# Experts of a hybrid network on one core: turning of the gates, second biases and their addition one half later, store one half later

## The chip, the cores and the metric

The kernel runs on one core of a Trainium2 chip. The metric is the device time in microseconds (us). Engines: PE (TensorE, matmuls and transposes; its weight loads are shown as PEld), DVE (VectorE), ACT (ScalarE), POOL (GpSimd) and SP (SyncE, which here only issues DMAs). Each engine works through a queue of its own in program order, and they wait for each other through semaphores.

## The reference

Eight pictures of 128 channels by 32 x 32 points pass through three layers. The first is an attention over the 1024 points of a picture, the second a state-space layer (a scan over the points), the third a mixture of eight experts. The change lies wholly in the third. Of the reference this is what matters (`t` holds the 1024 tokens of each picture, 128 values each):

```python
t = t + _L1_ffn_ref(_ln_t(t), router_w, w1, b1, w2, b2)

def _moe(tokens, router_w, w1, b1, w2, b2):
    logits = tokens @ router_w.T
    probs = softmax(logits)
    rw, re = top_k(probs, 2)
    rw = rw / maximum(rw.sum(-1), 1e-12)
    combine = zeros((N, 8)).at[arange(N)[:, None], re].set(rw)
    out = tokens
    for e in range(8):
        h = gelu(tokens @ w1[e] + b1[e])
        y = h @ w2[e] + b2[e]
        out = out + combine[:, e:e + 1] * y
    return out
```

All eight experts are computed for every token, in the reference and in the kernel. The second biases enter as `combine @ b2`.

## The kernel before

The three layers run one after the other over the eight pictures; the experts fill the last quarter of the program, from about 746 us. For each picture `b` the work of the experts is cut into 16 halves: half `n` is expert `n // 2` on tokens `512 * (n % 2)` and following. A half goes through these steps:

- PE, `expert` (lines 778 to 780): first product, three matmuls of 512 columns (high and low parts), into bank 4 or 5. It is issued two halves ahead.
- ACT, `gelu` (line 1378): the activation, into `hid[n % 2]`.
- PE, `second` (line 1028): second product, four matmuls, into bank 3, 6 or 7 in turn (half 15 uses bank 6, as half 13 does). It waits until `gelu` of that half is done and until DVE has added the half that used the bank before.
- DVE, `experts` (line 1970): four instructions add the gated product to `acc`. Each half added raises `e_added`.

So PE alternates: `second(n)`, `expert(n + 2)`, `second(n + 1)`, `expert(n + 3)`, and so on; `expert` of the last two positions belongs to the next picture. Below, 0', 1', ... are halves of the picture that follows in time.

Between the halves stands the preparation of the next picture, `b + 1`. In order: DVE takes the statistics of its tokens (after half 0), POOL makes the factors of the norm out of them (`norm`, lines 604 to 608), ACT normalizes (`token_norm`, line 1359, after half 5), PE turns the tokens (line 1040, after half 5), ACT and DVE split them into high and low parts (lines 1366 and 1896), PE computes the logits (after half 7), DVE finds the two largest and the gates (lines 1902 to 1938, after halves 7, 8, 10 and 11; the last writes `comb_s` and raises `e_gates_ready`). Then come the steps that the change moves:

- PE, `turn_weights` (line 1059): transposes the gates into bank 2. It waits for `e_gates_ready`.
- DVE, `turned` (line 1944): copies them to `comb_t` and raises `e_gates_copied`.
- PE, `second_biases` (line 1067): four matmuls of 512 columns, the gates times the second biases, into banks 0 and 1 (`lo_banks`). It waits for `e_gates_copied`.
- DVE, `biases` (line 1953): adds them to the next picture's `acc`.

The output of the picture before is turned by PE (`turn_out`, line 1077, after half 1; it waits for all 16 halves of that picture) into the same two banks, and ACT copies it to `o_ch` (`store`, line 1385), from where SP stores it to memory.

The order of every engine is written out by hand. Which step stands after which half is set by the comparisons `if n == ...` in the `experts` function of PE and ACT, and by the tuple of slots in that of DVE, which names the half after which each of the eight parts of `scores` runs: statistics, low, largest, places, softmax, weights, turned, biases. For the first picture these parts run inside the scan, by other lists, which stay as they are; so `experts` issues the turning seven times, for pictures 1 to 7.

Of the kernel before, what the change touches and what calls it, by code (L numbers as in the profile page):

```python
# [16 lines left out]
def hybrid_kernel(nc, x, x_tok, wqk, bqk, wv, bv_rows, wo2, bo, ident, fold, group_mean,  # L17
# [37 lines left out]
    with ExitStack() as ctx:  # L55
# [582 lines left out]
        def _(pe):  # L638
# [368 lines left out]
            def expert(b, u, n):  # L1007

                e, h = n // 2, n % 2
                if n >= 2 or not isinstance(b, int) or b > 0:  # L1010
                    pe.wait_ge(e_hidden_ready, 2 * NE * b + n - 1)
                pe.wait_ge(e_low_ready, b + 1)
                r = slice(h * BANK, (h + 1) * BANK)
                split(ps[:, 4 + n % 2, :], (w1_h[:, e, :], w1_l[:, e, :]),
                      (uh[u][:, r], ul[u][:, r])).then_inc(e_hidden_product, 1)

            def second(b, n, first):

                e, h = n // 2, n % 2
                pe.wait_ge(e_hidden_ready, 2 * NE * b + n + 1)  # L1020

                before = 3 if n < 2 * NE - 1 else 2
                if n >= 3:
                    pe.wait_ge(e_added, 2 * NE * b + n - before + 1)
                elif not first:
                    pe.wait_ge(e_added, 2 * NE * b - (3, 0, 1)[n])
                for t in range(4):
                    last = nc.tensor.matmul(ps[:, Y_BANKS[n], t * P:(t + 1) * P], hid[n % 2][:, t * P:(t + 1) * P],  # L1028
                                            w2_f[:, e, :], start=True, stop=True)
                last.then_inc(e_second_product, 1)  # L1030

            def turn_tokens(b):

                pe.wait_ge(e_normed, b + 1)
                if not isinstance(b, int) or b > 1:
                    pe.wait_ge(e_out_ready, b - 1)
                elif b == 1:
                    pe.wait_ge(e_bias_added, 1)
                for t in range(NT):
                    last = nc.tensor.transpose(cols(lo_banks, t, P), un[:, t, :], id_f[:])  # L1040
                last.then_inc(e_turned, 1)

            def logits(b, u):

                pe.wait_ge(e_low_ready, b + 1)
                if not isinstance(b, int) or b > 0:
                    pe.wait_ge(e_gates_copied, b)
                for t in range(NT):
                    r = slice(t * P, (t + 1) * P)
                    o = ps[:, 2, 2 * t * NE:2 * (t + 1) * NE]  # L1050
                    nc.tensor.matmul(o, uh[u][:, r], rw_s[:].rearrange("p k e -> p (k e)"), start=True, stop=False)
                    last = nc.tensor.matmul(o, ul[u][:, r], rw_s[:].rearrange("p k e -> p (k e)"), start=False, stop=True)
                last.then_inc(e_logits, 1)

            def turn_weights(b, u):

                pe.wait_ge(e_gates_ready, b + 1)
                pe.sem_inc(wait_carrier, 1)
                nc.tensor.transpose(ps[:, 2, P:2 * P], comb_s[u][:].rearrange("p k t e -> p (k t e)"),
                                    id_f[:]).then_inc(e_gates_turned, 1)  # L1060

            def second_biases(b):

                pe.wait_ge(e_gates_copied, b + 1)
                for h in range(2):
                    for part in range(2):
                        last = nc.tensor.matmul(lo_banks[:, h, :], comb_t[:], b2_s[:, part, h * BANK:(h + 1) * BANK],
                                                start=(part == 0), stop=(part == 1))
                last.then_inc(e_bias_product, 1)

            def turn_out(b, u):

                pe.wait_ge(e_added, 2 * NE * b + 2 * NE)
                if not isinstance(b, int) or b < B - 1:
                    pe.wait_ge(e_bias_added, b + 2)
                for t in range(NT):
                    done = nc.tensor.transpose(cols(lo_banks, t, P), acc[u][:, t, :], id_f[:])
                done.then_inc(e_sum_turned, 1)

            def experts(b, u, first, last):  # L1080
                for n in range(2 * NE):
                    second(b, n, first)
                    if n + 2 < 2 * NE:
                        expert(b, u, n + 2)
                    elif not last:
                        expert(b + 1, 1 - u, n + 2 - 2 * NE)
                    if n == 1 and not first:
                        turn_out(b - 1, 1 - u)
                    if not last:
                        if n == 5:  # L1090
                            turn_tokens(b + 1)
                        if n == 7:
                            logits(b + 1, 1 - u)
                        if n == 12:
                            turn_weights(b + 1, 1 - u)
                        if n == 13:
                            second_biases(b + 1)

            pe.wait_ge(attn_weights_loaded, 16 * 9)
# [49 lines left out]
        def _(act):  # L1149
# [202 lines left out]
            def token_norm(b):  # L1352

                act.wait_ge(e_shift_ready, 2 * b + 2)
                if not isinstance(b, int) or b > 0:
                    act.wait_ge(e_sum_started, b)
                    act.wait_ge(e_turned, b)
                for t in range(NT):
                    last = nc.scalar.activation(un[:, t, :], X[:, b, t * P:(t + 1) * P], ACT.Identity,  # L1359
                                                bias=enb[:, t:t + 1], scale=ers[:, t:t + 1])  # L1360
                last.then_inc(e_normed, 1)

            def token_high(b, u):

                act.wait_ge(e_turned, b + 1)
                nc.scalar.activation(two(uh[u][:]), lo_banks, ACT.Copy).then_inc(e_high_ready, 1)
# [6 lines left out]
            def gelu(b, n):  # L1373

                act.wait_ge(e_hidden_product, 2 * NE * b + n + 1)
                if n >= 2 or not isinstance(b, int) or b > 0:
                    act.wait_ge(e_second_product, 2 * NE * b + n - 1)
                nc.scalar.activation(hid[n % 2][:], ps[:, 4 + n % 2, :], ACT.Gelu,  # L1378
                                     bias=b1_f[:, n // 2:n // 2 + 1]).then_inc(e_hidden_ready, 1)

            def store(b, u):

                act.wait_ge(e_sum_turned, b + 1)
                act.wait_ge(out_free, b + 1)
                nc.scalar.activation(two(o_ch[u][:]), lo_banks, ACT.Copy).then_inc(e_out_ready, 1)

            def experts(b, u, first, last):
                for n in range(2, 2 * NE):
                    gelu(b, n)
                    if n == 3 and not first:  # L1390
                        store(b - 1, 1 - u)
                    if not last:
                        if n == 5:
                            token_norm(b + 1)
                        if n == 7:
                            token_high(b + 1, 1 - u)
                        if n == 9:
                            gate_exponentials(b + 1)
                if not last:
                    gelu(b + 1, 0)  # L1400
                    gelu(b + 1, 1)
# [40 lines left out]
        def _(dve):  # L1442
# [513 lines left out]

            def experts(b, u, first, last):

                parts = dict(zip((0, 5, 7, 8, 10, 11, 12, 13), scores(b + 1, 1 - u))) if not last else {}
                dve.wait_ge(e_bias_added, b + 1)  # L1960
                dve.wait_ge(e_gates_ready, b + 1)
                for k in range(2 * NE):
                    e, h = k // 2, k % 2
                    dve.wait_ge(e_second_product, 2 * NE * b + k + 1)
                    if k >= 2:
                        dve.wait_ge(e_added, 2 * NE * b + k - 1)
                    bank = (3, 6, 7)[k % 3] if k < 2 * NE - 1 else 6
                    for t in range(4):
                        tt = 4 * h + t
                        done = nc.vector.scalar_tensor_tensor(acc[u][:, tt, :], ps[:, bank, t * P:(t + 1) * P],  # L1970
                                                              comb[u][:, tt, e:e + 1], acc[u][:, tt, :],
                                                              ALU.mult, ALU.add)
                    done.then_inc(e_added, 1)
                    if k in parts:
                        parts[k]()
# [119 lines left out]
```

## Time and profile before

| | |
|---|---|
| median of 3 runs | 1012.92 us |
| lowest, highest | 1011.82, 1015.36 us |
| profiled execution, span | 1012.5 us |
| PE busy | 879.7 us, 87% |
| DVE busy | 740.6 us, 73% |
| ACT busy | 522.8 us, 52% |
| POOL busy | 250.1 us, 25% |
| mean granted TensorE clock | 0.938 |

The span runs from the first to the last instruction of one profiled execution; the profile states no other time of that execution than this span. A row of a timeline gives the start, the length, the engine and line, what is written and what is read, and in brackets how long the engine had been idle and who released it. Lengths of matmuls that follow each other overlap, so the distance from start to start tells how long one holds the engine. Shares of busy time are averages over the whole program; here only the stretch of the experts matters.

### The profile page before, as it was taken

What the parts mean: (1) busy time and instruction counts of PE and PEld (TensorE: products, weight loads), DVE (VectorE), ACT (ScalarE), POOL (GpSimd) and SP (SyncE); (2) the same over time, 40 slices, a digit from 0 to 9 for tenths busy, and PEclk for the clock granted to TensorE, in tenths of its full rate; (3) what the DMA queues carried; (4) which work ended last, traced back from release to release, by engine and by line L of the source; (5) the groups of instructions that cost most, each with busy time, mean ns of one, the idle gap of its engine ahead of it and who ended that gap; (6) DMA issues with size and microseconds to landing.
All of it is one profiled execution on the core that took longest, in us unless ns stands there. A gap on an engine that the chain in (4) does not pass through costs nothing.

```text
span 1012.5 us, 19616 instructions
## 1 busy us (share of the span) xinstructions
PE 879.7 (87%) x7534; PEld 686.5 (68%) x7534; DVE 740.6 (73%) x1959; ACT 522.8 (52%) x796; POOL 250.1 (25%) x250
## 2 busy tenths in 40 slices
PE   3788999999988797979787979798779899989997
PEld 2556565656575675867566767676568788878887
DVE  2867677767766768696859595856968877878785
ACT  1525445544577465646464646453334665456543
POOL 0035111011100534343325252527520111011100
PEclk9879999999999697989799989899999999999999
DMA  5531000000003030302030303031000000000000
GB/s 146 177 134 22 11 11 21 22 11 12 21 1 67 7 73 5 70 20 54 10 64 2 73 2 73 2 73 64 2 1 1 22 22 22 1 22 22 22 3 40
DMA packets 30892, 36.13 MB, mean 36 GB/s; under 512 B 4560, under 2 KB 24912, under 8 KB 30800
## 3 DMA queue, kind: packets, MB, share of 16 engines
q1 hardware_dynamic: 29648, 30.68, 12.4%
q10 hardware_dynamic: 1152, 4.19, 1.1%
q8 instruction: 61, 1.00, 0.4%
q14 instruction: 31, 0.25, 0.1%
HBM read 21.50 MB, written 4.98 MB: 26 GB/s over the span
## 4 chain that ended last, share of the span: by engine, by line
PE 60%; DVE 25%; ACT 6%; issue 5%; POOL 2%; SPq 0%; DMA 0%; DVEq 0%; ACTq 0%; POOLq 0%
PE ps L1028 7%; PE ps L699 6%; DVE cacc L1693 4%; PE ps L950 4%; PE ps L686 4%; PE ps L778 3%; DVE acc L1970 3%; PE ps L780 3%; PE ps L779 3%; PE ps L653 3%; PE ps L941 2%; PE ps L658 2%; ACT un L1359 2%; PE ps L934 2%; PE ps L675 2%
## 5 line engine op out<-in xcount | busy, mean ns | idle before, releaser
L1970 DVE SCALAR_TENSOR_TENSOR acc<-ps,comb,acc 128x128 f32<-128x128 f32 x512 | 141.2, 344 | 22.2 <-PE ps L1028 21.7
L1028 PEld LDWEIGHTS ps<-w_f,hid 128*128 128x128 f32 x1024 | 131.2, 191 | 16.2 <-ACT hid L1378 8.0
L1378 ACT ACTIVATE hid<-ps,b_f 128x512 f32<-128x512 f32 x128 | 86.1, 685 | 107.5 <-PE ps L780 107.4
L1028 PE MATMUL ps<-w_f,hid 128*128 128x128 f32 x1024 | 136.8, 276 | 4.6 <-ACT hid L1378 4.6
L569 POOL TENSOR_TENSOR srs<-sve,neg_half 128x1 f32<-128x1 f32 x64 | 50.8, 794 | 217.3 <-DVE gram L1802 217.3
L1550 DVE TENSOR_REDUCE nmax<-ps 128x1 f32<-128x1024 f32 x64 | 78.1, 1221 | 30.7 <-PE ps L658 30.4
L1693 DVE SCALAR_TENSOR_TENSOR cacc<-ps,cw,cacc 128x1023 f32<-128x1023 f32 (+5 forms) x72 | 91.8, 1275 | 10.4 <-ACT cacc L1250 9.6
L1319 ACT ACTIVATE dcy<-ps 128x1024 f32<-128x1024 f32 x64 | 65.0, 1016 | 59.0 <-PE ps L901 58.9
L1166 ACT ACTIVATE probs<-ps,nmax 128x1024 f32<-128x1024 f32 x64 | 71.2, 1113 | 38.7 <-DVE nmax L1550 35.8
L1785 DVE SCALAR_TENSOR_TENSOR dcy<-dcy,g_sb 128x1024 f32<-128x1024 f32 x64 | 86.1, 1346 | 0.1
L686 PEld LDWEIGHTS ps<-id_f,probs 128*128 128x128 f32 x512 | 59.9, 144 | 33.1 <-issue 23.5
L1172 ACT ACTIVATE pt<-ps 128x512 f32<-128x512 f32 x64 | 38.1, 595 | 77.4 <-PE ps L686 76.9
L686 PE MATMUL ps<-id_f,probs 128*128 128x128 f32 x512 | 69.8, 280 | 8.8 <-ACT pt L1172 6.7
L950 PE MATMUL ps<-y_w 128*128 128x256 f32 x256 | 74.4, 417 | 3.3 <-DVE X L1812 2.8
L1845 DVE TENSOR_TENSOR y_w<-ps,zs 128x256 f32<-128x256 f32 x64 | 27.0, 422 | 64.4 <-PE ps L941 46.8
L517 POOL TENSOR_TENSOR rs<-bve,neg_half 128x16 f32<-128x16 f32 x8 | 23.2, 2901 | 166.0 <-DVE bve L1598 166.0
L1555 DVE COPY pt<-ps 128x512 f32<-128x512 f32 x64 | 43.9, 686 | 27.7 <-PE ps L686 27.4
L699 PE MATMUL ps<-pt,v_f 128*64 128x512 f32 x256 | 64.1, 615 | 0.0
L950 PEld LDWEIGHTS ps<-y_w 128*128 128x128 f32 x256 | 51.7, 208 | 15.7 <-issue 2.9
L778 PE MATMUL ps<-uh,w_h 128*128 128x512 f32 x128 | 61.1, 477 | 0.0
L653 PE MATMUL ps<-k_a,q_a 128*128 128x512 f32 x128 | 48.5, 462 | 6.1 <-ACT probs L1166 4.4
L1250 ACT ACTIVATE cacc<-ps,cb,cw 128x1024 f32<-128x1024 f32 x24 | 28.9, 1204 | 48.0 <-PE ps L780 47.9
(212 smaller groups left out, 1905.0 us busy)
## 6 DMA issues: line engine op xcount, KB each, us to landing
c_dec<-exp_dram SPq DMA_DIRECT2D x32, 256.0 KB, 5.2
xc<-in_x SPq DMA_DIRECT2D x8, 512.0 KB, 3.6
q_b<-q_a SPq DMA_DIRECT2D x16, 256.0 KB, 2.8
X<-in_x_tok ACTq DMA_DIRECT2D x8, 512.0 KB, 5.5
c_rep<-cacc SPq DMA_DIRECT2D x32, 128.0 KB, 3.1
out<-o_ch SPq DMA_DIRECT2D x8, 512.0 KB, 2.6
w_f<-in_w SPq DMA_DIRECT2D x2, 512.0 KB, 4.2
cst_f<-in_sel_rows SPq DMA_DIRECT2D x1, 512.0 KB, 4.5
```

Source lines behind the costliest of these rows:

```text
L653: nc.tensor.matmul(S[j % 2][:, h, :], q_a[u][:, j * P:(j + 1) * P], k_a[u][:, h * BANK:(h + 1) * BANK], start=True, stop=False)
L686: last = nc.tensor.transpose(T[:, h, k * P:(k + 1) * P], probs[:, j % 2, (4 * h + k) * P:(4 * h + k + 1) * P], id_f[:])
L699: last = nc.tensor.matmul(O[e * DV:(e + 1) * DV, h, :], v_f[u][:, k, :], pt[:, k, h * BANK:(h + 1) * BANK], start=(quarter == 0), stop=(qu ...
L778: nc.tensor.matmul(o, lhs[0], rhs[0], start=True, stop=False)
L950: last = nc.tensor.matmul(ps[:, 6 + n % 2, DI:BANK].rearrange("p (k t) -> p k t", k=2), y_w[:, g, k, :], y_w[:, g, k:5:4 - k, :], start=(g ...
L1028: last = nc.tensor.matmul(ps[:, Y_BANKS[n], t * P:(t + 1) * P], hid[n % 2][:, t * P:(t + 1) * P], w2_f[:, e, :], start=True, stop=True)
L1166: nc.scalar.activation(probs[:, j % 2, :].rearrange("p (a n) -> p a n", a=2), S[j % 2], ACT.Exp, bias=nmax[:, j:j + 1], accum_out=rsum[u][ ...
L1378: nc.scalar.activation(hid[n % 2][:], ps[:, 4 + n % 2, :], ACT.Gelu, bias=b1_f[:, n // 2:n // 2 + 1]).then_inc(e_hidden_ready, 1)
L1550: nc.vector.tensor_reduce(nmax[:, j:j + 1], S[j % 2], AX_XY, ALU.max, negate=True).then_inc(max_ready, 1)
L1693: ins = nc.vector.scalar_tensor_tensor(cacc[b % 3][0:rows, g, k:N], banks[:, 0:N - k], cw[0:rows, g, DCONV - 1 - k:DCONV - k], cacc[b % 3] ...
L1785: nc.vector.scalar_tensor_tensor(mix[n % 3][:], dcy[n % 3][:], 1.0, g_sb[u][:, c:c + 1, :].to_broadcast([P, NH, P]), ALU.min, ALU.mult).th ...
L1970: done = nc.vector.scalar_tensor_tensor(acc[u][:, tt, :], ps[:, bank, t * P:(t + 1) * P], comb[u][:, tt, e:e + 1], acc[u][:, tt, :], ALU.m ...
```

## The change

Four numbers change. In the experts of every picture, PE turns the next picture's gates after half 13 where it did so after half 12, and computes the second biases after half 14 where it did so after half 13. DVE adds these biases after half 14 where it did so after half 13; its copy of the turned gates stays after half 12. ACT stores the output of the picture before after half 4 where it did so after half 3.

```diff
@@ PE, experts
                         if n == 7:
                             logits(b + 1, 1 - u)
-                        if n == 12:
+                        if n == 13:
                             turn_weights(b + 1, 1 - u)
-                        if n == 13:
+                        if n == 14:
                             second_biases(b + 1)
@@ ACT, experts
                     gelu(b, n)
-                    if n == 3 and not first:
+                    if n == 4 and not first:
                         store(b - 1, 1 - u)
@@ DVE, experts
-                parts = dict(zip((0, 5, 7, 8, 10, 11, 12, 13), scores(b + 1, 1 - u))) if not last else {}
+                parts = dict(zip((0, 5, 7, 8, 10, 11, 12, 14), scores(b + 1, 1 - u))) if not last else {}
```

On PE, around the turning of the gates (line 1059) in the first picture's experts; `hid` and `w_f` are the operands of a second product, `uh`, `ul`, `w_h`, `w_l` those of a first product:

```order
 L780 MATMUL ps<-uh,w_l 128x512
+L1028 MATMUL ps<-w_f,hid 128x128 x4
+L778 MATMUL ps<-uh,w_h 128x512
+L779 MATMUL ps<-ul,w_h 128x512
+L780 MATMUL ps<-uh,w_l 128x512
 L1059 MATMUL ps<-id_f,comb_s 128x128
 L1028 MATMUL ps<-w_f,hid 128x128 x4
```

A second product and a first product (half 13, and half 15 ahead) now stand in front of the turning. The same pair leaves the place behind the biases; farther on, before the output of the picture before is turned (line 1077):

```order
 L779 MATMUL ps<-ul,w_h 128x512
 L780 MATMUL ps<-uh,w_l 128x512
-L1028 MATMUL ps<-w_f,hid 128x128 x4
-L778 MATMUL ps<-uh,w_h 128x512
-L779 MATMUL ps<-ul,w_h 128x512
-L780 MATMUL ps<-uh,w_l 128x512
 L1077 MATMUL ps<-id_f,acc 128x128 x8
 L1028 MATMUL ps<-w_f,hid 128x128 x4
```

The turning, the pair behind it and the four matmuls of the biases keep their order among themselves; they have moved back by one pair as a block.

On DVE, from the sum of half 12 to the statistics of the picture after; line 1944 copies the turned gates and line 1953 adds the biases:

```order
 L1970 SCALAR_TENSOR_TENSOR acc<-ps,comb,acc 128x128 x4
 L1944 CAST comb_t<-ps 128x128
-L1970 SCALAR_TENSOR_TENSOR acc<-ps,comb,acc 128x128 x4
+L1970 SCALAR_TENSOR_TENSOR acc<-ps,comb,acc 128x128 x8
 L1953 TENSOR_TENSOR acc<-ps,acc 128x1024
-L1970 SCALAR_TENSOR_TENSOR acc<-ps,comb,acc 128x128 x12
+L1970 SCALAR_TENSOR_TENSOR acc<-ps,comb,acc 128x128 x8
 L1886 BN_STATS est<-X 128x6 x8
```

The addition of the biases has moved from between the sums of halves 13 and 14 to between those of 14 and 15. The copy has not moved.

On ACT, from the exponentials of the gates (`tex`) to the token norm (`un`), before:

```order
L1371 ACTIVATE tex<-tsh 128x64
L1378 ACT_TABLE_LOAD
L1378 ACTIVATE hid<-ps,b_f 128x512 x10
L1385 ACTIVATE o_ch<-ps 128x1024
L1378 ACTIVATE hid<-ps,b_f 128x512 x2
L1359 ACTIVATE un<-X,enb,ers 128x128 x8
L1378 ACTIVATE hid<-ps,b_f 128x512 x2
```

and now:

```order
L1371 ACTIVATE tex<-tsh 128x64
L1378 ACT_TABLE_LOAD
L1378 ACTIVATE hid<-ps,b_f 128x512 x11
L1385 ACTIVATE o_ch<-ps 128x1024
L1378 ACTIVATE hid<-ps,b_f 128x512
L1359 ACTIVATE un<-X,enb,ers 128x128 x8
L1378 ACTIVATE hid<-ps,b_f 128x512 x2
```

The copy to `o_ch` now stands between the activations of halves 4 and 5, of which the latter is the last ahead of the token norm.

## Rows read from the trace of the kernel before

**Rows 1.** The page, part 1: busy time and share of each engine.
```profile
PE 879.7 (87%) x7534; PEld 686.5 (68%) x7534; DVE 740.6 (73%) x1959; ACT 522.8 (52%) x796; POOL 250.1 (25%) x250
```

**Rows 2.** Busy time by engine in one picture's stretch, granted clock, DMA share, GB/s.
```profile
841.00:874.50 33.50, 30.79 (x213) 27.45 (x213) 27.40 (x128) 18.61 (x29) 4.41 (x4) 1.00 0.04 17
```

**Rows 3.** Waits from 775 to 978 us: total, times, longest.
```profile
PE ps L1059 <- DVE comb_s L1938: 9.1, 6, 1.5
PE ps L1040 <- ACT un L1359: 4.0, 6, 0.7
```

**Rows 4.** Idle time before line 1059, from 774 to 975 us: total, times.
```profile
  DVE comb_s L1938: 10.7, 7
```

**Rows 5.** Timeline of PE around a turning: start, length, operation, [idle before, releaser].
```profile
872.77 0.40 PE L780 MATMUL ps<-uh,w_l 128*128 128x512 f32 x1
874.69 0.30 PE L1059 MATMUL ps<-id_f,comb_s 128*128 128x128 f32 x1 [1.52 <-DVE comb_s L1938]
874.84 1.13 PE L1028 MATMUL ps<-w_f,hid 128*128 128x128 f32 x8
875.73 0.48 PE L778 MATMUL ps<-uh,w_h 128*128 128x512 f32 x1
876.27 0.39 PE L780 MATMUL ps<-uh,w_l 128*128 128x512 f32 x1
876.50 1.08 PE L1067 MATMUL ps<-b_s,comb_t 128*128 128x512 f32 x4
877.43 1.05 PE L1028 MATMUL ps<-w_f,hid 128*128 128x128 f32 x8
879.02 1.05 PE L1028 MATMUL ps<-w_f,hid 128*128 128x128 f32 x8
```

**Rows 6.** Timeline of DVE, the same stretch and the start of the next picture.
```profile
874.32 0.22 DVE L1938 TENSOR_TENSOR comb_s<-comb,comb_h 128x64 f32<-128x64 f32 x1
874.46 1.12 DVE L1970 SCALAR_TENSOR_TENSOR acc<-ps,comb,acc 128x128 f32<-128x128 f32 x4
875.50 0.28 DVE L1944 CAST comb_t<-ps 128x128 fp32r<-128x128 f32 x1
876.01 1.13 DVE L1970 SCALAR_TENSOR_TENSOR acc<-ps,comb,acc 128x128 f32<-128x128 f32 x4 [0.23 <-PE ps L1028]
877.69 1.23 DVE L1953 TENSOR_TENSOR acc<-ps,acc 128x1024 f32<-128x1024 f32 x1 [0.56 <-PE ps L1067]
878.84 1.12 DVE L1970 SCALAR_TENSOR_TENSOR acc<-ps,comb,acc 128x128 f32<-128x128 f32 x4
880.11 1.13 DVE L1970 SCALAR_TENSOR_TENSOR acc<-ps,comb,acc 128x128 f32<-128x128 f32 x4 [0.16 <-PE ps L1028]
881.79 1.12 DVE L1970 SCALAR_TENSOR_TENSOR acc<-ps,comb,acc 128x128 f32<-128x128 f32 x4 [0.56 <-PE ps L1028]
...
885.37 3.19 DVE L1970 SCALAR_TENSOR_TENSOR acc<-ps,comb,acc 128x128 f32<-128x128 f32 x12
```

**Rows 7.** Timeline of ACT: four halves' activations, the store, the token norm.
```profile
871.61 0.69 ACT L1378 ACTIVATE hid<-ps,b_f 128x512 f32<-128x512 f32 x1 [0.91 <-PE ps L780]
...
884.85 1.02 ACT L1385 ACTIVATE o_ch<-ps 128x1024 f32<-128x1024 f32 x1 [0.18 <-PE ps L1077]
886.43 0.69 ACT L1378 ACTIVATE hid<-ps,b_f 128x512 f32<-128x512 f32 x1 [0.56 <-PE ps L780]
888.02 0.69 ACT L1378 ACTIVATE hid<-ps,b_f 128x512 f32<-128x512 f32 x1 [0.90 <-PE ps L780]
888.60 3.18 ACT L1359 ACTIVATE un<-X,enb,ers 128x128 f32<-128x128 f32 x8
```

**Rows 8.** Timeline of ACT in the scan: two 128x1024 activations in a row.
```profile
719.42 1.02 ACT L1366 ACTIVATE uh<-ps 128x1024 fp32r<-128x1024 f32 x1 [0.34 <-PE ps L1040]
720.34 1.02 ACT L1319 ACTIVATE dcy<-ps 128x1024 f32<-128x1024 f32 x1
```

**Rows 9.** Timeline of POOL: the last step of the token norm's factors.
```profile
887.54 0.20 POOL L608 TENSOR_TENSOR enb<-enb,neg_one 128x8 f32<-128x8 f32 x1
```


## The prediction

> **What bounds the kernel now.** I began with the page's busy times: PE is the busiest engine over the program [rows 1], but that is an average over three layers, and the change lies in the last. So I cut the experts into one stretch per picture with the view by windows. In such a stretch (841.0 to 874.5 us) PE is busy 30.8 us, DVE 27.4, ACT 18.6, and TensorE is granted its full clock, 1.00 (2.4 GHz) [rows 2]. PE therefore sets the pace, and what a change is worth is read from PE's idle time. The view of waits names that: per picture PE waits 1.5 us for the gates at line 1059 and 0.7 us for the normalized tokens at line 1040 [rows 3]. The first is the one that the change touches. It occurs in all seven pictures of the experts, 10.7 us of shown idle time together [rows 4].
>
> The timeline shows why. The last matmul of the pair ahead of the turning starts at 872.77 [rows 5]. One such matmul holds PE for 876.50 - 876.27 = 0.23 us [rows 5], so PE is free at 873.00. The turning needs `comb_s`, which DVE begins to write for the last time at 874.32 and has ready at 874.54 [rows 6]. The turning starts at 874.69. So PE stands still for 1.69 us in front of it (the row shows 1.52, since it counts from the modelled end of the last matmul). Behind the turning in PE's queue stands half 13, which needs nothing of the gates.
>
> **PE: the turning one pair later.** What half 13 needs is there before 873.00. Its activation starts at 871.61 [rows 7] and takes 0.69, so it ends at 872.30. Its bank was last read by the sum of half 10, which DVE has done before it works on the gates. The half's weights and inputs are long loaded. So at 873.00 PE now starts the pair (second product 13, first product 15). A pair not held up takes 879.02 - 877.43 = 1.59 us [rows 5]. It ends at 874.59. The turning is still let go by the gates at 874.69, since nothing in front of them on DVE moves. PE idles 0.10 us where it idled 1.69. The turning holds PE for 0.15 us (874.84 - 874.69), as before.
>
> From 874.84 on the kernel before runs pair (13, 15), the biases, pair (14, 0'), pair (15, 1'), pair (0', 2'). The changed kernel runs pair (14, 0'), the biases, pair (15, 1'), pair (0', 2'). The durations: the pair behind the turning 876.50 - 874.84 = 1.66, the biases 877.43 - 876.50 = 0.93 [rows 5]. So half 15 starts at 877.43, half 0' at 879.02 and half 1' at 880.61. Before, half 0' started one pair after half 15, that is 879.02 + 1.59 = 880.61. The gain is one pair, 1.59 us for each picture, if no other wait appears. Seven pictures give 11.1 us.
>
> **What is late next: DVE.** This is where the gain could be lost, because the pairs now come sooner than DVE's sums were paced before. I follow DVE's queue. The sum of half 12 starts at 874.46, the copy of the turned gates at 875.50 [rows 6], so one sum of four instructions holds DVE for 1.04 us. The turning ends at 874.69 + 0.30, ahead of 875.50: the copy does not wait, though PE issues the turning after half 13 now and DVE's copy stays ahead of half 13. The copy takes 0.28. Then:
> - sum 13: at 875.78, without the 0.23 us wait that the row has [rows 6], since its product was made before the turning. It ends its hold at 876.82.
> - sum 14: its product is ready 876.01 - 874.84 = 1.17 us after its start at 874.84, at 876.01, so DVE goes on at once, 876.82 to 877.86.
> - biases: the product starts at 876.50, and before, the addition began 877.69 - 876.50 = 1.19 us after that [rows 5, 6]. That gives 877.69, so again no wait. It holds DVE for 878.84 - 877.69 = 1.15 us, to 879.01.
> - sum 15: 879.01, shown length 1.13 [rows 6], ends 880.14.
>
> On PE half 15 uses bank 6 again, as half 13 does: it needs sum 13 (about 876.91) at 877.43. Half 1' uses bank 6 after half 15: it needs sum 15 (880.14) at 880.61. The margins are 0.52 and 0.47 us. The second is the tightest. For half 0' the sum starts 881.79 - 880.61 = 1.18 us after its product [rows 5, 6] (880.61 is worked out above), so at 880.20, and DVE is free for it at 880.05. From there the next picture is in the same phase as before, all 1.59 us earlier: the statistics, POOL's factors, the token norm. DVE has its waits of 0.56 us ahead of sum 0' before and 0.15 after, so its queue does not fall behind. Of the cover that is used up, POOL's is untouched: it has the factors at 887.74 [rows 9], and the token norm starts at 888.60 [rows 7], 0.86 us later.
>
> How sure is the run of five pieces without a pause? Taken at their shown lengths with no overlap (0.28 + 3 x 1.13 + 1.23) it is 4.90 us instead of 4.64, which leaves 0.21 of the margin. That three sums in a row take 3.19 us is seen [rows 6]. Cost taken: 0; bounds 0 and the upper case in the rivals.
>
> **ACT: the store one half later.** Before, it starts at 884.85, takes 1.02 and is over well ahead of the activation of half 4' at 886.43 [rows 7]; it delayed nothing, so nothing is won by taking it away. In its new place: after half 4' ACT can take the next instruction 888.60 - 888.02 = 0.58 us later [rows 7], at 887.01 in the old clock. Two activations of this size from PSUM follow each other after 720.34 - 719.42 = 0.92 us [rows 8]. So ACT is free at 887.93, and half 5' is due at 888.02. Margin 0.09, cost 0. By the full 1.02 us it is 0.01 us late. This counts one to one, since PE waits for the token norm right behind it [rows 3], in six pictures: at most 0.1 us. SP's DMA of the output starts some 2 us later, with nothing behind it that waits. The last store of the program is the same as before.
>
> [...]
>
> **Sum.** 7 x 1.59 = 11.1 won, 0 to 0.1 lost. From the profiled span, 1012.5 - 11.1 = 1001.4 us. The median of the runs is 1012.92, 0.4 above the span, so the forecast in the metric is 1001.8 us. The most that can be won is 7 x 1.69 = 11.8 (1001.1), when PE never waits for the gates.
>
> **Rivals.**
> - *Part is given back at bank 6.* DVE's stretch from the copy to the end of sum 15 stays as long as it is before: 875.50 to 880.11 + 1.13 = 881.24 [rows 6], its waits for PE included. Half 1' would then start 881.24 - 880.61 = 0.63 us late, in seven pictures 4.4 us: 1006.2. For it: the margin is only 0.47 us. Against: the waits in that stretch (0.23, 0.56, 0.16 [rows 6]) are for PE, and PE is ahead now.
> - *No gain: half 13 can't start before the gates.* If half 13 starts at T, nothing is lost up to T = 873.10, and nothing won from T = 874.69. Then 1012.9. Against: both things that it waits for are done by 872.30.
> - *Slower: DVE sets the pace.* If every instruction in the stretch held the next one for as long again (a pause that the pacing by PE hides now), the stretch would be 9.3 instead of 4.64 us, 4.2 over the margin, 29 us in seven pictures, and with 11.1 won 1031. It turns slower from a stretch of 4.64 + 0.47 + 1.59 = 6.70 us. Against: sums in a row at 1.04 us and the biases' hold of 1.15 with a length of 1.23 [rows 6]: the next instruction starts before the shown end. The Trainium skill, VectorE: DVE Perf Modes, section "The DRAIN you can't avoid", says that each DVE operation is followed by a flush of its length less 266 ns before the next may start. If that came on top of the shown length it would add about 0.3 us to each sum and 0.96 to the biases, a stretch near 6.5, and nearly all of the gain would be gone; the trace has it inside the shown length.
>
> **How the numbers follow.** The forecast has 0.84, and by itself it spans 999.8 to 1004: 1.1 us around the sum for the margins and the rest for the spread of runs (before: 1011.8 to 1015.4). Giving back a part has 0.09, no gain 0.04, slower 0.03. The range for 8 in 10 is 999.5 to 1005.5. The bound between faster and same is 0.3% (3 us), about what a measurement of this kernel can tell from no change. Faster: 0.84 + 0.09 = 0.93 less 0.01 for a bad spread, 0.92; same 0.05; slower 0.03.
>
> **What would show it.** In the changed profile: the wait for `comb_s` at line 1059 falls from 1.5 to about 0.1 us or less in seven pictures (that of the first picture, in the scan, stays); DVE from the copy to sum 15 has no wait for line 1028 or line 1067; the distance from one picture's turning to the next falls by 1.6 us; clock 1.00. The prediction is wrong if line 1028 begins to wait for line 1970 (bank 6), if line 1378 ahead of the token norm comes right behind line 1385 and later than due, or if the wait at line 1040 grows beyond 0.7 us.

## The result, and the profile after

The changed kernel took 999.82 us (median of 4 runs, 998.84 to 1002.53), the kernel before 1013.99 us (median of 4 runs, 1011.82 to 1015.36). The ratio is 0.9874 with a 95% interval of 0.9836 to 0.9912: faster by 1.3%, clear of the 0.3% below which the prediction calls two times the same. The prediction was 1001.8 us with a range of 999.5 to 1005.5.

The profiled run took 1000.13 us with a span of 998.1 us. First the waits of PE, as a list of who waited for whom (total, times, longest), in the changed kernel from the first picture of the experts on:

```profile
PE ps L1040 <- ACT un L1359: 4.8, 7, 0.8
PE ps L1028 <- ACT hid L1378: 4.6, 8, 1.4
PE ps L1077 <- DVE acc L1970: 1.2, 1, 1.2
```

The wait of line 1059 for `comb_s` [rows 3, 4] is no longer among them. The other three have the same totals as the kernel before has over its own stretch of the experts. Next PE's timeline around one turning, in the columns of [rows 5]:

```profile
864.91 1.05 PE L1028 MATMUL ps<-w_f,hid 128*128 128x128 f32 x8
...
866.27 0.40 PE L780 MATMUL ps<-uh,w_l 128*128 128x512 f32 x1
866.60 0.30 PE L1059 MATMUL ps<-id_f,comb_s 128*128 128x128 f32 x1
866.75 1.13 PE L1028 MATMUL ps<-w_f,hid 128*128 128x128 f32 x8
...
868.41 1.10 PE L1067 MATMUL ps<-b_s,comb_t 128*128 128x512 f32 x4
869.35 1.05 PE L1028 MATMUL ps<-w_f,hid 128*128 128x128 f32 x8
870.94 1.05 PE L1028 MATMUL ps<-w_f,hid 128*128 128x128 f32 x8
872.53 1.05 PE L1028 MATMUL ps<-w_f,hid 128*128 128x128 f32 x8
```

Half 13 starts at 864.91 and the turning at 866.60, 1.69 us later: the pair of 1.59 us fills the place where PE stood, and 0.10 us are left. Behind it come half 14, the biases, half 15, half 0' and half 1', at the distances that [rows 5] have, to 0.01 us. From one picture's turning to the next it is 31.9 us (834.71 to 866.60), where it was 33.4 (841.27 to 874.69): the 1.6 us that the prediction named as its sign.

DVE in the same stretch, to be held against [rows 6]:

```profile
866.23 0.23 DVE L1938 TENSOR_TENSOR comb_s<-comb,comb_h 128x64 f32<-128x64 f32 x1
866.37 1.12 DVE L1970 SCALAR_TENSOR_TENSOR acc<-ps,comb,acc 128x128 f32<-128x128 f32 x4
867.41 0.28 DVE L1944 CAST comb_t<-ps 128x128 fp32r<-128x128 f32 x1
867.60 2.15 DVE L1970 SCALAR_TENSOR_TENSOR acc<-ps,comb,acc 128x128 f32<-128x128 f32 x8
869.67 1.21 DVE L1953 TENSOR_TENSOR acc<-ps,acc 128x1024 f32<-128x1024 f32 x1
870.80 1.12 DVE L1970 SCALAR_TENSOR_TENSOR acc<-ps,comb,acc 128x128 f32<-128x128 f32 x4
872.13 1.13 DVE L1970 SCALAR_TENSOR_TENSOR acc<-ps,comb,acc 128x128 f32<-128x128 f32 x4 [0.21 <-PE ps L1028]
```

From the copy on there is no wait up to sum 0'. The stretch from the copy to the end of sum 15 is 871.92 - 867.41 = 4.51 us, and half 1', which needs it, starts at 872.53, 0.61 us later. ACT and POOL at the new place of the store, against [rows 7] and [rows 9]:

```profile
876.77 0.69 ACT L1378 ACTIVATE hid<-ps,b_f 128x512 f32<-128x512 f32 x1 [1.76 <-PE ps L780]
877.35 1.02 ACT L1385 ACTIVATE o_ch<-ps 128x1024 f32<-128x1024 f32 x1
878.36 0.69 ACT L1378 ACTIVATE hid<-ps,b_f 128x512 f32<-128x512 f32 x1
878.94 3.18 ACT L1359 ACTIVATE un<-X,enb,ers 128x128 f32<-128x128 f32 x8
```

```profile
877.89 0.20 POOL L608 TENSOR_TENSOR enb<-enb,neg_one 128x8 f32<-128x8 f32 x1
```

Half 5' comes 1.59 us after half 4', one pair: the store delays nothing that can be seen. The factors of the norm are there at 878.09, 0.85 us before it starts.

The stretches: busy time of PE, PEld, DVE, ACT, POOL, then granted clock. The kernel before first, cut at the start of the first second product (747.6 us), then the changed kernel, cut at the same instruction (744.3 us):

```profile
650.00:747.60 97.60, 76.87 (x1019) 59.44 (x1007) 69.77 (x181) 37.17 (x55) 45.01 (x49) 0.93 0.15 36
747.60:1012.50 264.90, 240.99 (x1669) 215.23 (x1669) 209.10 (x946) 141.51 (x219) 30.90 (x28) 1.00 0.04 17
```

```profile
650.00:744.30 94.30, 74.94 (x1002) 59.05 (x1002) 67.16 (x177) 34.63 (x49) 44.05 (x47) 0.93 0.15 37
744.30:998.10 253.80, 240.53 (x1669) 215.12 (x1669) 207.16 (x946) 140.65 (x219) 30.96 (x28) 1.00 0.05 18
```

The experts take 253.8 us where they took 264.9: 11.1 us less, with PE's busy time the same (241.0 and 240.5). The other 3.3 of the 14.4 us between the two spans lie ahead of the experts, where no instruction was changed. From here on "the stretch" is this distance, from the first second product to the end of the span.

### The profile page after: what moved, and what is told of

Same layout as the page of the kernel before. It is cut to its first block, busy times and chain, and to the rows that moved or that the text cites. A ratio compares the mean times of both kernels' runs of the same rounds, so it can differ in the third digit from the quotient of the medians.

```text
span 998.1 us, 19616 instructions
## 1 busy us (share of the span) xinstructions
PE 877.9 (88%) x7534; PEld 688.2 (69%) x7534; DVE 738.8 (74%) x1959; ACT 522.0 (52%) x796; POOL 250.4 (25%) x250
## 4 chain that ended last, share of the span: by engine, by line
PE 64%; DVE 20%; ACT 7%; issue 5%; POOL 2%; SPq 0%; DMA 0%; DVEq 0%; ACTq 0%; POOLq 0%
PE ps L1028 9%; PE ps L699 6%; DVE cacc L1693 5%; PE ps L778 4%; PE ps L950 4%; PE ps L686 4%; PE ps L780 4%; PE ps L779 4%; PE ps L653 3%; PE ps L658 2%; PE ps L941 2%; ACT un L1359 2%; PE ps L675 2%; PE ps L934 2%; DVE dcy L1785 2%
## 5 line engine op out<-in xcount | busy, mean ns | idle before, releaser
L901 PE MATMUL ps<-rhs_c,lhs_c 128*128 128x512 f32 x128 | 47.5, 454 | 7.8 <-ACT dcy L1319 7.8
## 6 DMA issues: line engine op xcount, KB each, us to landing
c_dec<-exp_dram SPq DMA_DIRECT2D x32, 256.0 KB, 5.3
q_b<-q_a SPq DMA_DIRECT2D x16, 256.0 KB, 2.8
```

## The experiments

Times are medians, ratios are to the kernel before on the same chip, with their 95% interval. The diffs are against the kernel before unless said otherwise; `(12, 13)` on DVE are the last two of its slots.

**The kernel before again.** No edit.

> The kernel before, unchanged, as a control. From the first second product (line 1028) to the end of the span it took 264.9 us in the profile of before and 253.8 us in that of the changed kernel; the part ahead of it took 747.6 and 744.3 us although no instruction there was changed. Theory (the part ahead of the experts varies by some us from one execution to the next, and the change has nothing to do with it): this run shows a part ahead that differs from 747.6 by up to 3 us, and a stretch of experts within 0.3 us of 264.9. Rival (the change shortened the part ahead too): this run shows 747.6 within 0.5 us, and the changed kernel stays near 744.3 when it is run again.

Measured: ratio 1.0005 (0.9982 to 1.0028); stretch 1008.6 - 743.6 = 265.0 us; part ahead 743.6 us. Over the profiled runs of kernels that are the same up to the experts the part ahead came out between 738.7 and 747.6 us. That is a wider spread than the 3 us I had put down. The theory holds in kind: 3.3 us are well inside the spread of the part ahead, and the stretch does not contain that part.

**The block alone.**

```diff
-turn_weights at n == 12, second_biases at n == 13; DVE slots (12, 13)
+turn_weights at n == 13, second_biases at n == 14; DVE slots (12, 14)
```

> Only the block of turning and second biases moved (PE after halves 13 and 14, the addition on DVE after half 14); the store stays after half 3. Theory (the whole gain is the pair in front of the turning): stretch of the experts 253.8 us, total 11 us below before. Rival (the late store carries part of the gain): less than 10 us below before.

Measured: 1000.46 us, ratio 0.9891 (0.9850 to 0.9932); stretch 999.0 - 745.2 = 253.8 us, as in the changed kernel. The block carries the whole gain.

**The store alone.**

```diff
-                    if n == 3 and not first:
+                    if n == 4 and not first:
```

> Only the store on ACT moved, from after half 3 to after half 4. Theory (it fits into ACT's idle time in both places): stretch of the experts 264.9 to 265.0 us, time as before within 0.2 us. Rival (it holds up the activation of half 5 and the token norm): up to 1 us longer. Rival (its old place cost something): shorter by 0.5 us or more.

Measured: 1011.79 us, ratio 0.9997 (0.9978 to 1.0016); stretch 1003.7 - 738.7 = 265.0 us. The store's move is worth nothing in the stretch, in either direction. (The medians alone could not say so: their interval is some 2 us to either side.)

**The changed kernel again.** The block and the store.

> The changed kernel again, on the same chip as the other three. Theory: stretch of the experts 253.8 us within 0.3, total 11 us below before within 1; the part ahead of the experts lies in the same range as that of the unchanged kernel. Rival (13 to 14 us below before is the change's own work): the part ahead is again near 744.3 us and the total 13 us or more below.

Measured: 999.43 us, ratio 0.9877 (0.9838 to 0.9917); stretch 996.8 - 743.1 = 253.7 us. The medians are 12.2 us apart, and the interval spans 8 to 16 us: it holds the 11 us of the stretch, but could not tell them from 13 by itself. The part ahead is 743.1 us, next to the 743.6 of the unchanged kernel on the same chip, so that the change shortened the part ahead is not borne out, and the rival falls.

**The turning without the biases.**

```diff
-turn_weights at n == 12
+turn_weights at n == 13
```

> Of the change only the turning moves (PE, after half 13); the biases stay after half 13, right behind it, with their addition. On PE no pair stands between the turning and the biases any more, so PE waits for DVE's copy of the gates. Theory: the turning is free at 874.84 in the clock of the kernel before, the copy ready at 875.8, so about 1.0 us of new idle time ahead of line 1067 in each of seven pictures: the stretch of the experts takes about 260.4 us, 4.5 below before and 6.6 above the changed kernel. Rival (only the wait for the gates matters, the place of the biases is free): 253.8 us.

Measured: 1007.71 us, ratio 0.9956 (0.9930 to 0.9982); stretch 1005.7 - 744.7 = 261.0 us. PE's timeline:

```profile
837.24 0.30 PE L1059 MATMUL ps<-id_f,comb_s 128*128 128x128 f32 x1
838.38 1.21 PE L1067 MATMUL ps<-b_s,comb_t 128*128 128x512 f32 x4 [0.84 <-DVE comb_t L1944]
839.42 1.05 PE L1028 MATMUL ps<-w_f,hid 128*128 128x128 f32 x8
```

Without a pair between the turning and the biases PE stands for DVE's copy: 838.38 - 837.24 - 0.15 = 0.99 us in a picture. The four matmuls behind the stop hold PE 1.04 us and not 0.93, and the pair after them takes 1.59 and not 1.66: 1.03 us in all, 7.2 in seven pictures, as the stretch shows. I had 6.6. The gain shrinks from 11.1 to 3.9 us. So the biases have to move with the turning.

**The addition at its old place.** Against the changed kernel, with the store after half 3:

```diff
-DVE slots (12, 14)
+DVE slots (12, 13)
```

> The changed PE order, but DVE adds the biases after half 13 as before. Theory: DVE waits 0.9 us for the biases' product, sum 15 ends at 881.0 where half 1 of the next picture needs bank 6 at 880.6, so 0.4 to 0.5 us are lost per picture, 3.3 in all: the stretch of the experts takes about 257 us, with a wait of line 1028 for line 1970. Rival (the margin at bank 6 is larger than 0.47 us, or DVE is not what PE waits for): 253.8 us.

Measured: 1006.17 us, ratio 0.9926 (0.9893 to 0.9959); stretch 1000.0 - 742.0 = 258.0 us. DVE, and then PE at half 1':

```profile
834.67 1.12 DVE L1970 SCALAR_TENSOR_TENSOR acc<-ps,comb,acc 128x128 f32<-128x128 f32 x4
836.68 1.23 DVE L1953 TENSOR_TENSOR acc<-ps,acc 128x1024 f32<-128x1024 f32 x1 [0.89 <-PE ps L1067]
837.82 3.19 DVE L1970 SCALAR_TENSOR_TENSOR acc<-ps,comb,acc 128x128 f32<-128x128 f32 x12
```

```profile
838.00 1.05 PE L1028 MATMUL ps<-w_f,hid 128*128 128x128 f32 x8
...
840.12 1.13 PE L1028 MATMUL ps<-w_f,hid 128*128 128x128 f32 x8 [0.37 <-DVE acc L1970]
```

DVE waits 0.89 us as expected, and PE then waits for the sum at bank 6. Half 1' starts 2.12 us after half 0' and not 1.59: 0.53 us lost, and 0.07 more behind it, as behind the stop in [rows 5], where the pair takes 1.66 us and not 1.59. Seven times 0.60 is 4.2 us, which is what the stretch lost; my 3.3 had 0.47 for the stop and left out the 0.07. Sum 15 is the second of the three in DVE's last row, so by an estimate (837.82 + 2 x 1.04 + 0.08) it ends at 839.98, and PE starts 0.14 us later. The rows have the same distance [rows 5, 6]: `comb_s` is ready at 874.54, the turning starts at 874.69. The margin at bank 6 is real, and DVE's slot is what spares it.

**All of it two halves later.**

```diff
-turn_weights at n == 12, second_biases at n == 13; DVE slots (12, 13)
+turn_weights at n == 14, second_biases at n == 15; DVE slots (13, 15)
```

> Everything one more half later: PE turns the gates after half 14 and makes the biases after half 15, DVE copies after half 13 and adds after half 15; the store is after half 3. Theory: PE no longer idles the 0.1 us before the turning, but half 15 now stands right behind it and needs sum 13, which ends 0.25 us later than PE comes; net 0.15 us per picture worse than the changed kernel, 254.9 us for the stretch of the experts. Rival (PE's remaining idle time is won): 0.17 us per picture better, 252.6 us.

Measured: 1004.81 us, ratio 0.9909 (0.9876 to 0.9942); stretch 998.9 - 742.9 = 256.0 us. PE at half 15:

```profile
835.53 0.27 PE L1059 MATMUL ps<-id_f,comb_s 128*128 128x128 f32 x1
836.13 1.13 PE L1028 MATMUL ps<-w_f,hid 128*128 128x128 f32 x8 [0.33 <-DVE acc L1970]
```

The direction is right, the size was too small: 2.2 us over the changed kernel, 0.31 per picture, where I had 0.15. The stop is 836.13 - 835.53 - 0.15 = 0.45 us; I had 0.25. In DVE's timeline of this run sum 13 ends at 835.98, and PE starts 0.15 us after that. I had counted up to the sum's end and left this 0.15 us out. The 0.10 us before the turning is won, so 0.35 is lost by this count. (The pair behind the stop takes 1.65 us, but so it does behind the turning in the changed kernel.)

**The same, with the copy at its old place.** As the last one, but DVE slots `(12, 15)`.

> As the kernel with everything two halves late, but DVE's copy of the turned gates stays after half 12. DVE now stands at the copy while PE is still on the pair in front of the turning. Theory (an early place in DVE's queue holds up the sums behind it, and these hold up PE at bank 6): DVE waits about 1.0 us for line 1059, half 15 starts 1.6 us late, the stretch of the experts takes about 263.6 us, nearly as long as before. Rival (DVE has slack for it): 254.9 us or less.

Measured: 1010.64 us, ratio 0.9991 (0.9964 to 1.0018); stretch 1004.8 - 740.2 = 264.6 us. DVE, then PE:

```profile
835.56 0.29 DVE L1944 CAST comb_t<-ps 128x128 fp32r<-128x128 f32 x1 [0.89 <-PE ps L1059]
835.77 2.15 DVE L1970 SCALAR_TENSOR_TENSOR acc<-ps,comb,acc 128x128 f32<-128x128 f32 x8
```

```profile
835.25 0.27 PE L1059 MATMUL ps<-id_f,comb_s 128*128 128x128 f32 x1
837.03 1.13 PE L1028 MATMUL ps<-w_f,hid 128*128 128x128 f32 x8 [1.51 <-DVE acc L1970]
```

DVE stands at the copy, the sums behind it come late, and PE stops for sum 13. Against the kernel two halves late this costs 264.6 - 256.0 = 8.6 us. Nearly the whole gain is gone. In the changed kernel, where the turning is one half earlier, the same place of the copy costs nothing.

**Banks in turn, and all of it two halves later.** The banks 3, 6, 7 are taken in turn through all pictures, by PE and by DVE, so that a second product always needs the sum three halves before (line 1025 in these kernels is the second product, 1056 the turning, 1037 the turning of the tokens):

```diff
-            Y_BANKS = [(3, 6, 7)[n % 3] for n in range(2 * NE - 1)] + [6]
+            Y_BANKS = (3, 6, 7)
...
+                if n >= 3 or not first:
+                    pe.wait_ge(e_added, 2 * NE * b + n - 2)
...
+                    last = nc.tensor.matmul(ps[:, Y_BANKS[(2 * NE * b + n) % 3], t * P:(t + 1) * P], ...
```

> The kernel with turning, biases, copy and addition two halves later (store after half 3), and the banks 3, 6, 7 taken in turn through all pictures, so that half 15 no longer shares bank 6 with half 13: each second product needs the sum three halves before. Theory (what the kernel with everything two halves late lost was the wait for sum 13, and PE's 0.1 us before the turning and 0.07 us behind it are then won): 7 times 0.17 to 0.25 us below the changed kernel, the stretch of the experts 252.1 to 252.6 us. Rival (DVE is late in another place, at the biases): 253.8 us or more.

Measured: 998.16 us, ratio 0.9867 (0.9845 to 0.9890); stretch 996.1 - 743.9 = 252.2 us. No second product waits for a sum any more, and the stretch is 3.8 us shorter than that of the kernel two halves late and 1.6 below the changed kernel, 0.23 per picture. Of that the 0.10 us before the turning and the 0.07 behind it are 0.17. The turning itself now holds PE for 0.11 us instead of 0.15, which is 0.04 more. What is left, 0.2 us over all seven pictures, is also what the banks in turn alone bring in the next kernel; its cause is open.

**Banks in turn in the changed kernel.** The same three edits on the changed kernel.

> The changed kernel with the banks 3, 6, 7 taken in turn through all pictures. Theory (in the changed kernel no second product waits for a sum, so the banks' margin is worth nothing): the stretch of the experts 253.8 us within 0.2. Rival: half 1 of the next picture was held a little at bank 6, 253.5 us or less.

Measured: 999.44 us, ratio 0.9897 (0.9863 to 0.9931); stretch 994.6 - 741.0 = 253.6 us, within the 0.2 of the theory. It lies closer to 253.5 than to 253.8, so by itself it does not decide between the two. The list of waits of the changed kernel does: no second product waits for a sum there.

**The store right ahead of the token norm.** Against the changed kernel:

```diff
-                    if n == 4 and not first:
+                    if n == 5 and not first:
```

> The changed kernel with the store on ACT after half 5 instead of half 4, so right in front of the token norm. Theory (ACT has no room there, and PE waits for the token norm): the norm starts 0.92 us later in six pictures, the stretch of the experts 253.8 + 5.5 = 259.3 us. Rival (there is slack behind the token norm, so the place of the store hardly matters): 253.8 to 255 us.

Measured: 1004.96 us, ratio 0.9936 (0.9913 to 0.9958); stretch 1002.0 - 743.0 = 259.0 us. ACT, then PE:

```profile
847.57 1.02 ACT L1385 ACTIVATE o_ch<-ps 128x1024 f32<-128x1024 f32 x1
848.47 3.17 ACT L1359 ACTIVATE un<-X,enb,ers 128x128 f32<-128x128 f32 x8
```

```profile
851.70 1.09 PE L1040 MATMUL ps<-id_f,un 128*128 128x128 f32 x8 [1.57 <-ACT un L1359]
```

The store holds ACT 0.90 us, and PE's wait at line 1040 grows from 0.67 to 1.57 us, by the same 0.90. In six pictures that is 5.4 us; the stretch grew by 5.2. The Trainium skill, ScalarE: Activation LUTs, section "What ACT_TABLE_LOAD costs", gives 186 ns and 0.833 ns per element for an activation with immediate scale and bias, and an overlap of about 93 ns between two in a row. By an estimate from that page the store, which is of this kind, would be 1.04 us long and hold ACT for 0.95; the trace has 1.02 and 0.90. What ACT does right ahead of the token norm counts in full, and one half earlier it counts nothing.

**The wait for the token norm taken away.** With the banks in turn, the store after half 4, the whole preparation one half later, and the norm in two parts:

```diff
-                        if n == 5:
-                            token_norm(b + 1)
-                        if n == 7:
+                        if n in (5, 6):
+                            token_norm(b + 1, 4 * (n - 5), 4 * (n - 4))
+                        if n == 8:
                             token_high(b + 1, 1 - u)
-                        if n == 9:
+                        if n == 10:
                             gate_exponentials(b + 1)
...
+PE: turn_tokens at 6, logits at 8, turn_weights at 14, second_biases at 15
+DVE: slots (0, 6, 8, 9, 11, 12, 13, 15)
```

> As the kernel with rotated banks, and every step of the preparation from the turning of the tokens on one half later, the store after half 4; ACT normalizes four token tiles after half 5 and four after half 6, so that half 6 is activated between them. Theory: the wait of PE for the token norm (line 1040, 0.7 us shown, 0.84 with the modelled ends) goes too, in seven pictures about 5.9 us: the stretch of the experts about 248 us, 17 us below before. Rival (the token norm's delay comes back as a wait for the logits or the gates): 252 us or more.

Measured: 993.58 us, ratio 0.9831 (0.9807 to 0.9854); stretch 986.4 - 739.1 = 247.3 us, 6.5 below the changed kernel and 4.9 below the one with the banks in turn and all of it two halves later. ACT, and then PE's waits in the experts behind the first half (line 1376 is the activation here, 1356 the norm, 1025 the second product, 1074 the turning of the output):

```profile
838.52 0.69 ACT L1376 ACTIVATE hid<-ps,b_f 128x512 f32<-128x512 f32 x1
839.11 1.64 ACT L1356 ACTIVATE un<-X,enb,ers 128x128 f32<-128x128 f32 x4
840.65 0.67 ACT L1376 ACTIVATE hid<-ps,b_f 128x512 f32<-128x512 f32 x1
841.22 1.64 ACT L1356 ACTIVATE un<-X,enb,ers 128x128 f32<-128x128 f32 x4
```

```profile
PE ps L1025 <- ACT hid L1376: 3.1, 7, 0.4
PE ps L1074 <- DVE acc L1968: 1.2, 1, 1.2
```

The activation of half 6 between the two parts gives PE work while the second part runs. Both waits of [rows 3] are gone; of what PE waited for in each picture only the 0.4 us behind the exponentials is left. The 4.9 us are 0.70 per picture, where I had 0.84; what takes the rest is not shown. Nor is it shown which part of the 4.9 us belongs to the split and which to the later preparation, since this kernel changes both at once. This is the fastest of the kernels that ran.

## Why the prediction was right, and where it was off

- **PE sets the pace, and its idle time is the gain.** Right. With the clock at 1.00 and PE's busy time nearly unchanged (241.0 and 240.5 us) the stretch shrank by what PE stood still less: 1.59 of the 1.69 us per picture.
- **A pair takes the place of the wait: 1.59 us in seven pictures.** Right, 11.1 us predicted, 264.9 - 253.8 = 11.1 measured, and 11.1 to 11.3 in the repeats. The block of turning, biases and addition carries it alone.
- **DVE's queue keeps up.** Right. The stretch I put at 4.64 us took 4.51, the margin of 0.47 was 0.61; the copy gives way to the next sum 0.19 us after its start, and I had counted its full 0.28. But the margin compared the end of sum 15 with the start of half 1', and left out that PE starts some 0.15 us after the sum that it waits for, though 874.54 and 874.69 in the rows show this distance. The room was 0.32 us by the prediction's own times, and by the measured ones 0.46. Here nothing came of it; in the kernel two halves later the same omission made the stop 0.45 us where I had 0.25. That a loss waits close by is shown by the addition at its old place (4.2 us lost) and, in the kernel two halves late, by the copy at its old place (8.6 us lost).
- **The store costs 0 to 0.1 us and brings nothing.** Right: 265.0 against 264.9 us without the block, 253.8 against 253.8 with it. The store held ACT for 1.01 us in front of half 5' and 0.90 us in front of the norm; that half 5' waited for its product, due in the same hundredth, or for the store can't be told apart.
- **From the span to the metric.** This step was off. I put the time 0.4 us above the span because the median of three runs stood there. In the run profiled after the change it stands 2.0 us above (1000.13 and 998.1), and 1.76 to 2.16 in the others. By an estimate the profiled execution of before thus took some 1014.5 us, in the upper part of the spread, and the right sum from it is 1012.5 + 2.0 - 11.1 = 1003.4 us. That 1001.8 came nearer to the 999.82 is luck: the missing 1.6 us pulled the forecast down, and the part ahead of the experts, which the prediction had only as the spread of the runs, happened to be 3.3 us shorter in the profile after. The range held the time by 0.3 us, which is luck too: the unchanged kernel alone spread from 1006.3 to 1016.8 us in the runs of the experiments, more than the range is wide.
- **Rivals.** Giving back a part at bank 6 did not happen, but it is the mechanism that works as soon as DVE's slot is wrong. Half 13 was not held. DVE did not pause between the instructions of this stretch: from sum to copy are 1.04 us with a shown length of 1.12, from the biases to the next sum 1.13 with 1.21. The section of the Trainium skill that the prediction cites for a flush (VectorE: DVE Perf Modes, "The DRAIN you can't avoid") also says that an operation that is not held starts earlier. That fits these rows, where each starts 0.08 us before the shown end of the one in front. No row shows a flush by itself, so the prediction's word that it lies inside the shown length is its reading.

## What to carry to other kernels

Where an engine with a queue in program order waits for a result in a steady loop, measure the wait against the nearest independent piece behind it; if the piece fits, as 1.59 us did into 1.69, the gain is its full length, once per turn of the loop. Then follow every queue that takes part: the steps that use the result have to move with it (the biases), one at a time each costs a part of the gain (7.2 us without the biases' move, 4.2 with the addition too early), and moving on past the point where the wait has gone runs into the next resource, here a bank freed two halves before instead of three. In a margin count up to the start of the engine that is let go, not only to the end of the one that lets it go: the distance was some 0.15 us here. And compare stretches that hold the change, cut at an instruction, when the rest of the program spreads by more than the effect.

## What the runs showed of the hardware

Identical code ahead of the experts took 738.7 to 747.6 us in the profiled executions, while the experts' stretch came out at 264.9 and 265.0 us for the unchanged kernel, 265.0 with the store alone, and 253.7 and 253.8 for the changed kernel. The profile of the kernel with the store alone, two stretches of the scan and the experts:

```profile
500.00:650.00 150.00, 130.48 (x1590) 105.15 (x1589) 113.35 (x199) 87.05 (x127) 60.61 (x66) 0.91 0.18 38
650.00:738.70 88.70, 72.93 (x1000) 57.46 (x999) 63.06 (x170) 33.60 (x47) 42.20 (x46) 0.96 0.17 40
738.70:1003.70 265.00, 241.04 (x1669) 215.24 (x1669) 209.13 (x946) 140.68 (x219) 30.93 (x28) 1.00 0.04 17
```

In the scan the granted TensorE clock is 0.91 and 0.96 here, where the kernel before had 0.90 (from 500 to 650 us) and 0.93 (from there to the experts); in the experts it is 1.00 in both. The spread of the part ahead goes along with that clock only loosely. Over the last 250 us ahead of the experts the four profiled runs with the shortest part ahead (738.7 to 741.0 us) have 0.92 and the longest (747.6) has 0.91, but one at 743.0 has 0.92 too, and another 0.90. Where the spread comes from was not tested.

PE started 0.14 to 0.15 us after the DVE instruction that it waited for had ended: the turning in the kernel before (874.54 to 874.69), half 15 in the kernel two halves late (835.98 to 836.13), half 1' with the addition at its old place (839.98, an estimate, to 840.12). Where such a stop stood ahead of a pair, the pair took 1.65 or 1.66 us and not 1.59.
